# Cross-attention scores and values as three 128-column matmuls in one PSUM bank, in place of two of 256 columns with the halves added on VectorE

## The reference, cut to what matters

```python
    x = _rmsnorm(hidden_states, ln_weight)
    h_q = (x @ w_q.T).reshape(b, lq, H, DH)
    h_k = (key_value_states @ w_k.T).reshape(b, lk, H, DH)
    h_v = (key_value_states @ w_v.T).reshape(b, lk, H, DH)
    score = jnp.einsum('bqhd,bkhd->bhqk', h_q, h_k)
    score = score + position_bias[None]
    score = jnp.where(m, score, -jnp.inf)
    score = jax.nn.softmax(score, axis=-1)
    score = jnp.where(m, score, 0.0)
    attn = jnp.einsum('bqhk,bkhd->bqhd', score, h_v).reshape(b, lq, H * DH)
    return hidden_states + attn @ w_out.T
```

## Time and profile before

| what | value |
|---|---|
| median of 3 runs | 2133.66 us (2133.07 to 2134.09) |
| profiled execution, first to last instruction | 2132.0 us |
| TensorE busy | 2052.8 us, 96% |
| VectorE busy | 1501.1 us, 70% |
| ScalarE busy | 1017.1 us, 48% |
| GpSimd busy | 548.4 us, 26% |
| DMA queue, share of 16 engines | 11.8% |
| chain that ended last, share on TensorE | 87% |

### The profile page before, as it was taken

The page is one execution under the profiler, slowest core; times in us unless marked ns, Lnnn a source line. Parts: engine busy times, 40 slices in busy tenths (PEclk is TensorE's granted clock), DMA queues, the critical chain, the costliest instruction groups (busy, mean ns, idle before and its releaser), DMA issues.

```text
span 2132.0 us, 33393 instructions
## 1 busy us (share of the span) xinstructions
PE 2052.8 (96%) x11352; PEld 1763.7 (83%) x11352; DVE 1501.1 (70%) x2365; ACT 1017.1 (48%) x2232; POOL 548.4 (26%) x428
## 2 busy tenths in 40 slices
PE   5999999999999999999799999999999999988996
PEld 4888888888888888888688888888888888876885
DVE  6777777777777777777666666666666666677776
ACT  3555555555555555555454444444444444433331
POOL 2222122212221222221232222222222222223223
PEclk9999999999999999999999999999999999999998
DMA  7000000000000000011011111111111111010111
GB/s 233 16 21 16 16 20 20 15 15 20 20 16 14 20 20 20 12 48 40 30 59 42 40 37 40 39 38 42 42 42 42 42 42 42 23 35 25 49 44 50
DMA packets 44161, 76.87 MB, mean 36 GB/s; under 512 B 7379, under 2 KB 13651, under 8 KB 43603
## 3 DMA queue, kind: packets, MB, share of 16 engines
q1 hardware_dynamic: 44114, 76.25, 11.8%
HBM read 74.13 MB, written 2.10 MB: 36 GB/s over the span
## 4 chain that ended last, share of the span: by engine, by line
PE 87%; DVE 7%; issue 3%; ACT 2%; DMA 0%; SPq 0%; DVEq 0%; ACTq 0%
PE bank L1085 22%; PE bank L1087 22%; PE bank L1086 22%; PE bank L1145 9%; PE bank L1190 6%; PE bank L1258 1%; PE bank L1341 1%; PE bank L1259 1%; PE bank L1340 1%; PE bank L1315 1%; DVE negmax L870 1%; DVE V_lo L864 1%; DVE pT_lo L908 1%; DVE q_lo L902 1%; DVE stats L768 0%
## 5 line engine op out<-in xcount | busy, mean ns | idle before, releaser
L880 DVE SCALAR_TENSOR_TENSOR xacc<-bank,rinv,xacc 128x512 f32<-128x512 f32 x512 | 375.9, 745 | 71.5 <-PE bank L1087 71.3
L486 ACT ACTIVATE pT_hi<-bank 128x512 fp32r<-128x512 f32 x320 | 190.7, 597 | 202.4 <-PE bank L1190 202.1
L870 DVE TENSOR_REDUCE negmax<-bank 128x1 f32<-128x640 f32 x256 | 210.2, 821 | 37.2 <-PE bank L1145 30.0
L540 ACT ACTIVATE prob<-bank,negmax 128x640 f32<-128x640 f32 x256 | 202.6, 791 | 66.7 <-DVE negmax L870 66.7
L908 DVE TENSOR_TENSOR pT_lo<-bank,pT_hi 128x512 fp32r<-128x512 f32 x320 | 217.6, 680 | 2.4 <-ACT pT_hi L486 2.4
L1190 PE MATMUL bank<-ident,prob 128*128 128x128 f32 x1280 | 191.3, 272 | 0.0
L1190 PEld LDWEIGHTS bank<-ident,prob 128*128 128x128 f32 x1280 | 159.2, 140 | 18.7
L383 POOL TENSOR_TENSOR wo_lo<-wo_raw,wo_hi 128x512 fp32r<-128x512 f32 x32 | 41.4, 1293 | 428.4 <-ACT wo_hi L486 428.4
L1085 PE MATMUL bank<-xwv_hi,cT_hi 128*128 128x256 f32 x512 | 144.2, 282 | 3.1 <-DVE xV_lo L928 3.1
L626 ACT ACTIVATE xprob<-xscore,negmax 128x128 f32<-128x128 f32 x256 | 99.5, 391 | 95.9 <-DVE negmax L961 95.9
L1086 PE MATMUL bank<-xwv_lo,cT_hi 128*128 128x256 f32 x512 | 143.8, 281 | 0.0
(11 more groups left out here) (169 smaller groups left out, 5867.3 us busy)
## 6 DMA issues: line engine op xcount, KB each, us to landing
wq_raw<-in_wq SPq DMA_DIRECT2D x32, 256.0 KB, 2.6
wo_raw<-in_wo SPq DMA_DIRECT2D x32, 256.0 KB, 2.6
xwv_raw<-in_xwv SPq DMA_DIRECT2D x16, 512.0 KB, 3.3
xwk_raw<-in_xwk SPq DMA_DIRECT2D x32, 256.0 KB, 3.5
xwq_raw<-in_xwq SPq DMA_DIRECT2D x32, 256.0 KB, 3.4
xwo_raw<-in_xwo SPq DMA_DIRECT2D x32, 256.0 KB, 2.6
w_raw<-in_w SPq DMA_DIRECT2D x32, 256.0 KB, 2.6
xacc<-in_x SPq DMA_DIRECT2D x8, 256.0 KB, 4.6
```

Source lines behind the costliest of these rows:

```text
L486: return s.activation(dst, src, ACT.Copy)
L540: s.activation(prob[:, slot, i, :].rearrange("p (a t) -> p a t", a=2), S_bank[i % 2], ACT.Exp, bias=negmax[:, slot, i:i + 1], scale=1.0, a ...
L870: v.tensor_reduce(negmax[:, slot, i:i + 1], S_bank[i % 2], mybir.AxisListType.XY, ALU.max, negate=True).then_inc(a["max"], 1)
L880: v.scalar_tensor_tensor(xacc[:, 4 * half + i, :], M, rinv[:, k, i:i + 1], xacc[:, 4 * half + i, :], ALU.mult, ALU.add).then_inc(sems["y"], 1)
```

## The change

Scores and values are issued through `mm3`, three matmuls of 128 columns a sequence, `hi*hi`, `hi*lo`, `lo*hi`, all into the same 128 columns of PSUM. A step's four sequences then fill one bank. The scores alternate between banks 0 and 1 by the parity of the step; the values are in bank 3 alone, apart from the transposes' bank 2. The additions of halves, the tile `xo`, one copy on ScalarE and the semaphores `c_s1`, `ohi` and `osum` are gone, and with them TensorE's wait before the transposes. The product `lo*lo`, which the 256-column form computed along with the rest, isn't computed any more.

```diff
-        XS_bank = bank[:, 0:2, :].rearrange("p b (t n) -> p (b t) n", t=2)
-        XO_bank = bank[:, 2:4, :].rearrange("p b (t n) -> p (b t) n", t=2)
+        XS_bank = [bank[:, i, :].rearrange("p (t n) -> p t n", t=4) for i in range(2)]
+        XO_bank = bank[:, 3, :]
@@ scalar, c_step
                 act.wait_ge(c["pv"], n + 1)
-                copy(xo[:, 0], XO_bank[:, :, 0:P]).then_inc(c["ohi"], 1)
-                act.wait_ge(c["osum"], n + 1)
-                copy(xoT_hi[:, k].rearrange("p (t n) -> p t n", t=4), xo[:, 1]).then_inc(c["oThi"], 1)
+                copy(xoT_hi[:, k], XO_bank).then_inc(c["oThi"], 1)
@@ vector, c_score
-                v.tensor_tensor(xscore[:, slot], XS_bank[:, :, 0:P], comb[:, half], ALU.add).then_inc(c_s1, 1)
-                dve.wait_ge(c_s1, n + 1)
-                v.tensor_tensor(xscore[:, slot], XS_bank[:, :, P:2 * P], xscore[:, slot], ALU.add)\
-                 .then_inc(c["score"], 1)
+                v.tensor_tensor(xscore[:, slot], XS_bank[slot], comb[:, half], ALU.add).then_inc(c["score"], 1)
@@ vector, c_step
                 acc(1)
-                dve.wait_ge(c["ohi"], n + 1)
-                v.tensor_tensor(xo[:, 1], XO_bank[:, :, P:2 * P], xo[:, 0], ALU.add)\
-                 .then_inc(c["osum"], 1)
                 if not more1:
                     acc(2)
                 dve.wait_ge(c["oThi"], n + 1)
-                v.tensor_tensor(xoT_lo[:, k].rearrange("p (t n) -> p t n", t=4), xo[:, 1],
-                                xoT_hi[:, k].rearrange("p (t n) -> p t n", t=4),
-                                ALU.subtract).then_inc(c["oTlo"], 1)
+                v.tensor_tensor(xoT_lo[:, k], XO_bank, xoT_hi[:, k], ALU.subtract).then_inc(c["oTlo"], 1)
@@ tensor, c_scores
                 for i in range(4):
                     cols = slice(i * P, (i + 1) * P)
-                    t.matmul(XS_bank[:, i, :], xq_hi[:, k, cols], xk[:, k, i], start=True, stop=False)
-                    last = t.matmul(XS_bank[:, i, :], xq_lo[:, k, cols], xk[:, k, i], start=False, stop=True)
+                    last = mm3(XS_bank[k][:, i, :], [z[:, k, cols] for z in (xq_hi, xq_lo)],
+                               [xk[:, k, i, e, :] for e in range(2)], True, True)
@@ tensor, c_step
                 pe.wait_ge(c["exp"], 4 * n + 4)
-                if not first:
-                    pe.wait_ge(c["osum"], n)
@@ tensor, c_step
                 for i in range(4):
-                    t.matmul(XO_bank[:, i, :], xV_hi[:, k, i, hp * P:(hp + 1) * P], xpT[:, i], start=True, stop=False)
-                    last = t.matmul(XO_bank[:, i, :], xV_lo[:, k, i, hp * P:(hp + 1) * P], xpT[:, i],
-                                    start=False, stop=True)
+                    last = mm3(XO_bank[:, i * P:(i + 1) * P], [z[:, k, i, hp * P:(hp + 1) * P] for z in (xV_hi, xV_lo)],
+                               [xpT[:, i, e, :] for e in range(2)], True, True)
```

More of the change, by code:

```diff
@@ L119, in decoder_layer @@
                 xpT = sb(lo_, "xpT", [P, 4, 2, P], F32R)
-                xo = sb(lo_, "xo", [P, 2, 4, P])
                 xoT_hi, xoT_lo = pair(lo_, "xoT", [P, 2, HALF])
@@ L157, in decoder_layer @@
         s_xl, s_factor = sem("centred_weighted"), sem("factors_made")
-        a_rot1, c_r1, c_s1 = sem("a_rot_products"), sem("c_reciprocal"), sem("c_score_hi")
+        a_rot1, c_r1 = sem("a_rot_products"), sem("c_reciprocal")
         a = {n: sem("a_" + n) for n in (
@@ L168, in decoder_layer @@
             "qwhi", "qwlo", "kwhi", "kwlo", "vwhi", "vwlo", "owhi", "owlo", "comb", "S", "score", "max", "exp",
-            "tr", "pThi", "pTlo", "pv", "ohi", "osum", "oThi", "oTlo", "q", "qhi", "qlo", "k", "khi", "klo", "v", "vhi", "vlo",
+            "tr", "pThi", "pTlo", "pv", "oThi", "oTlo", "q", "qhi", "qlo", "k", "khi", "klo", "v", "vhi", "vlo",
             "rinv", "wo", "y", "res")}
```

## The result

The changed kernel takes 2178.42 us (median of 4 runs, 2176.30 to 2178.62) against 2133.36 us (4 runs, 2131.31 to 2134.09). The ratio is 1.0214, interval 1.0200 to 1.0229: 45 us slower. The forecast was 2177 us.

A forecast was written before the change was run, and what follows sets the result against it. The prediction took TensorE's program-order stream to bound the kernel: span 2132.0 us, plus 48.1 for load-bound 128-column matmuls, minus 5 at the stage's ends, gives 2175.1; with 1.7 for the median, 2177 us. Range 2166 to 2372 us.

The forecast's parts named there:

- TensorE's stream is the bound: Cross-attention stage: nearly all TensorE work in program order, busy 846.2 of 852 us, so only changes to its stream count.
- The forecast's list of TensorE's waits: Around the stage: single waits of 1.8 us for `xo`, 1.4 for `xk`, 3.3 for the first `xT_lo`, none repeated per step.
- A 128-column matmul costs 110 ns, its load: Score and value groups: the weight load sets the pace, 12 x 110 = 1320 ns against 944, +48.1 us over 128 groups.
- The alternatives in the range and outside it (233, 60, 79 to 83 ns): Price per 128-column matmul: four passes (2367 us, chance 0.36), streaming (2100 us, 0.07), balance (about 2134 us, 0.05).
- The exit costs no more: End of each group: the next matmul's load follows at the same distance, already in the twelfth gap, so nothing extra.
- VectorE's and ScalarE's relief is hidden but for the ends: Stage: 88 us less VectorE and 38 us less ScalarE work, worth nothing in steady steps, 5 us at start and end.
- The clock stays up: Cross-attention stage: TensorE's granted clock is 1.00, the 2.4 GHz level; no term for a change of it.
- The forecast's sign of being wrong: Stage: the prediction counts as wrong if TensorE's granted clock falls there.
- No new wait, nothing late in its place: Steady steps: two waits go, none is added; producers get earlier or stay while TensorE gets later.
- Sum: Whole kernel: span 2132.0 + 48.1 - 5 = 2175.1 us, with 1.7 for the median 2177 us, 2.0% slower.
- The low end of the range: Forecast time: 2166 us, said to allow loads at 105 ns and 6 us at the ends.
- The four-pass rival: Score and value groups: 128-column matmuls take four passes, 233 ns each, +237 us, 2367 us; chance 0.36 for above 118 ns.

The follow-up runs named there:

- narrow: Changed kernel with the second and third matmul of each three cut to 64 streamed columns, same weight loads: 2176.24 us, ratio to before 1.0216.
- halfload: Changed kernel with 128x64 weights in all twelve matmuls of a group, still streaming 128 columns: 2102.31 us, ratio to before 0.9864.
- mixed: Kernel before with the second matmul of each pair cut from 256 to 128 columns, so lo*lo is left out: 2130.56 us, ratio 0.9993.
- two: Changed kernel without the second matmul (hi*lo) of each three: 2121.16 us, ratio to before 0.9955.
- interleave: Changed kernel with the value matmuls and the 512-column key projection matmuls issued in turn: 2195.32 us, ratio to before 1.0300.
- relief: Kernel before, 256-column matmuls kept, without the second score addition, the addition of value halves and one ScalarE copy: 2126.93 us, ratio 0.9972.
- mixed_tail: Kernel before with mixed in all steps, except the 128-column form in the last scores and last two value groups: 2124.88 us, ratio 0.9968.

## Why the prediction was right

- *TensorE's stream is the bound.* Right: +46.6 us busy, +44.3 us of span, no waits in the steady steps. The forecast's list of TensorE's waits left one out, 3.1 us for `xacc` in two waits at the stage's end; after the change it is 2.0.
- *A 128-column matmul costs 110 ns, its load.* Right in mechanism and size: 111 to 112, and 1334 ns a group (944 + 390) against the forecast's 1320. The 14 ns make 1.8 us over 128 groups. The alternatives in the range and outside it (233, 60, 79 to 83 ns) are excluded by that distance itself. That it is the load and not the streaming is shown by narrow and halfload, and mixed, two and interleave agree.
- *The exit costs no more.* Right as a sum, wrong as drawn: at a value group the entry shows 50 ns less and the exit 47 more.
- *VectorE's and ScalarE's relief is hidden but for the ends.* Right in the steady steps, where it is worth 0.9 us in all. At the ends the size was right partly by luck. The forecast had 6 us, 2.7 at the start (two score additions and `xo` with its copy) and 3.3 at the end, and took 5. Relief alone shows 4.5 by the medians (2131.46 to 2126.93). In its profile the end is 4.7 us shorter, by the estimate above 1.9 of that from the clock, a term that the forecast doesn't have. The start is 0.6 us shorter: from the stage's first `xT_lo` to the transposes of step 4 it is 72.9 us before and 72.3 with relief, with the granted clock at 0.79 in both from 1057 to 1065 us. So the start's 2.7 was mis-sized and the end's excess made up for it.
- *The clock stays up.* Nearly. In the stage's steady part it is 1.00 in both kernels. From 1057 to 1065 us it is 0.79 before and 0.57 after, and near the end it is 0.52 for 7 us before and 1.00 after. The forecast's sign of being wrong, a clock that falls in the stage, is met only in those 8 us at its start.
- *No new wait, nothing late in its place.* Right in the steady steps.
- *Sum.* 2132.0 + 48.1 - 5 = 2175.1 stood against a span of 2176.3. By the steady distance the groups cost 49.9, so the rest gave back 5.6. The low end of the range is 2 us too low by its own terms: 105 ns a load and 6 us at the ends give 2168, not 2166.
- *Chances.* The four-pass rival had 0.36, on the ground that no row showed a non-transposing matmul so narrow. That was fair to the rows, but the earlier trace rows both give 110 ns, as finely as they are printed, and might have carried more.

## What to carry to other kernels

A matmul costs the greater of its streaming and one weight load: here 0.45 ns a moving column against 111 ns for 128 columns of weights, which cross at some 240 moving columns by calculation; no width between 128 and 256 was run. Below that, don't count columns, count loads. Two matmuls of 256 columns that compute an unneeded quarter are cheaper than three of 128 that don't. Take a VectorE saving at full value only where the chain of waits runs over it; here that was mostly the last four steps of 64, and a special form for the last scores and the last two value groups kept the gain almost without the price. At such ends compare the granted clock as well, before a gain is put down to the work removed.

## What the runs showed of the hardware that was not expected

- The records of matmuls don't show a short stall where it arises. After a narrow matmul the next record starts 60 ns on and is lengthened (0.34 in place of 0.28 us for 256 columns, 0.44 to 0.46 in place of 0.39 for 512). Sum over a round of the pattern; a single distance of starts misleads, as the 60 ns in mixed and interleave would have.
- The granted clock at the stage's start and end differs from one execution to another, and between kernels with the same code there: mixed_tail takes 1.4 us longer than mixed from the first `xT_lo` to the transposes of step 4 (73.9 against 72.6), with the clock at 0.57 and 0.79 from 1057 to 1065 us.
- Weight loads of 64 columns follow each other at 60 ns, those of 128 at 110, and repeating the same weights saves nothing: in the changed kernel the second matmul of each three has the weights of the first, they are loaded again, and its distance to the next is 110 to 112 ns like the others'.
